# Random features of a linear-attention transformer computed as sixteen 32x32 TensorE tiles, with up and down pieces moved around them

## What is computed

```python
h = _layernorm(x) * (1 + ca) + sa
x = x + ga * attn_ref(h, ...)          # the first half of the kernel
h = _layernorm(x) * (1 + cb) + sb
return x + gb * ffn_ref(h, ...)        # the second half

def favor(x, omega):                   # dh = 16, m = 16, omega is 16 x 8
    xs = x * dh ** (-0.25)
    u = einsum('bshd,dm->bshm', xs, omega)
    h = 0.5 * sum(xs * xs, axis=-1, keepdims=True)
    return concatenate([exp(u - h), exp(-u - h)], axis=-1) * m ** (-0.5)

for l in range(3):                     # 16 heads of 16
    q, k, v = out @ Wq[l] + bq[l], out @ Wk[l] + bk[l], out @ Wv[l] + bv[l]
    Qf, Kf = favor(q, omega[l]), favor(k, omega[l])
    a = causal_linear_attention(Qf, Kf, v) @ Wo[l] + bo[l]
    h = layer_norm(out + a, ln1_g[l], ln1_b[l])
    y = relu(h @ W1[l] + bf1[l]) @ W2[l] + bf2[l]     # 256 -> 1024 -> 256
    out = layer_norm(h + y, ln2_g[l], ln2_b[l])
```

## Time and profile before

| | before |
|---|---|
| runs | 2620.6, 2623.1, 2625.83 us; median 2623.1 us |
| profiled execution | 2624.48 us, span of the instructions 2622.7 us |
| busy share of the span | PE 97%, DVE 81%, ACT 59%, POOL 54% |
| mean granted TensorE clock | 0.993 |
| chain that ended last | PE 90%, DVE 4%, issue 3%, ACT 2%, POOL 1% |

### The profile page before, as it was taken

The page is one execution under the profiler, slowest core; times in us unless marked ns, Lnnn a source line. Parts: engine busy times, 40 slices in busy tenths (PEclk is TensorE's granted clock), DMA queues, the critical chain, the costliest instruction groups (busy, mean ns, idle before and its releaser), DMA issues.

```text
span 2622.7 us, 63564 instructions
## 1 busy us (share of the span) xinstructions
PE 2545.6 (97%) x22368; PEld 2096.2 (80%) x22368; DVE 2119.8 (81%) x5244; ACT 1545.4 (59%) x3137; POOL 1423.9 (54%) x1406
## 2 busy tenths in 40 slices
PE   7899999999999999999898999999999999999998
PEld 4688888888888888887776788888888887888876
DVE  5788877887777787888899888878898887888775
ACT  3544455445544554455246777777777777776772
POOL 2244344443444345445476756656676666776664
PEclk9999999999999999999999999999999999999999
DMA  3100000010000010000111100000111100110001
GB/s 91 38 18 10 18 2 17 14 36 2 1 2 13 15 39 10 18 26 25 52 38 56 29 17 12 19 16 14 35 32 35 31 27 23 35 32 27 28 29 48
DMA packets 78985, 67.32 MB, mean 26 GB/s; under 512 B 15800, under 2 KB 73272, under 8 KB 78680
## 3 DMA queue, kind: packets, MB, share of 16 engines
q1 hardware_dynamic: 78680, 63.25, 8.1%
HBM read 49.18 MB, written 12.58 MB: 24 GB/s over the span
## 4 chain that ended last, share of the span: by engine, by line
PE 90%; DVE 4%; issue 3%; ACT 2%; POOL 1%; SPq 0%; DMA 0%; DVEq 0%; ACTq 0%; POOLq 0%
PE PS L274 79%; PE PS L984 4%; PE PS L946 1%; PE PS L1014 1%; PE PS L937 1%; PE PS L487 1%; PE PS L477 1%; PE PS L425 1%; PE PS L895 1%; DVE PS L3586 1%; DVE U L3178 1%; PE PS L1044 0%; ACT PR L2246 0%; DVE SQ L3566 0%; SPq L5388 0%
## 5 line engine op out<-in xcount | busy, mean ns | idle before, releaser
L2246 ACT ACTIVATE PR<-PS,SM 128x256 f32<-128x256 f32 (+1 forms) x512 | 280.3, 559 | 136.5 <-DVE SM L3591 136.0
L1932 ACT ACTIVATE FB<-PS,BC 128x512 f32<-128x512 f32 x192 | 133.4, 695 | 323.0 <-PE PS L274 184.7
L3178 DVE TENSOR_TENSOR U<-PS,CST 128x512 f32<-128x512 f32 x384 | 238.2, 683 | 34.2 <-PE PS L274 33.9
L4618 POOL TENSOR_TENSOR RL<-FB,RH 128x512 fp32r<-128x512 f32 x96 | 126.0, 1312 | 219.9 <-DVE RH L3155 219.9
L274 PE MATMUL PS<-W2H,RH 128*128 128x256 f32 x768 | 226.1, 294 | 6.7 <-POOL RL L4618 6.6
L4840 POOL TENSOR_TENSOR SM<-SM,COL 128x8 f32<-128x8 f32 x128 | 223.8, 1748 | 10.7
L3586 DVE CUSTOM_DVE_ANT_0 PS<-PS,MSK 128x256 f32<-128x256 f32 (+1 forms) x512 | 202.6, 436 | 29.4 <-PE PS L274 28.2
L274 PE MATMUL PS<-W2H,RL 128*128 128x256 f32 x768 | 215.9, 281 | 0.0
L274 PE MATMUL PS<-W2L,RH 128*128 128x256 f32 x768 | 215.8, 281 | 0.0
L4630 POOL TENSOR_TENSOR SBD<-SBD,TMP 128x256 f32<-128x256 f32 x84 | 64.3, 766 | 207.3 <-DVE TMP L3170 207.3
L274 PEld LDWEIGHTS PS<-W2H,RH 128*128 128x128 f32 x768 | 145.1, 189 | 29.5 <-issue 24.9
(11 more groups left out here) (265 smaller groups left out, 8535.6 us busy)
## 6 DMA issues: line engine op xcount, KB each, us to landing
PX<-in_L_attn_x SPq DMA_DIRECT2D x16, 512.0 KB, 3.6
TB<-in_k_rot SPq DMA_DIRECT2D x64, 128.0 KB, 2.1
SG<-in_L_attn_W SPq DMA_DIRECT2D x24, 256.0 KB, 2.7
xp_scratch<-PX SPq DMA_DIRECT2D x8, 512.0 KB, 2.9
xs_scratch<-X SPq DMA_DIRECT2D x64, 64.0 KB, 1.5
ZS<-xs_scratch SPq DMA_DIRECT2D x16, 256.0 KB, 2.8
GG<-xp_scratch SPq DMA_DIRECT2D x7, 512.0 KB, 3.8
out<-GG SPq DMA_DIRECT2D x7, 512.0 KB, 2.9
```

The lines of the kernel that those rows point to most:

```text
L1932: e.activation(FB[:, hb % 2, :], PS[:, 5, :], ACT.Relu, bias=BC[:, l % 2, 4 + hb:5 + hb]).then_inc(*a_re.up(n, hb))
L2246: t = e.activation(PR[:, par, 256 * i + lo:256 * i + hi], PS[:, 3 + par, 256 * i + lo:256 * i + hi], ACT.Exp, bias=S[:, 40 + 2 * g + i:41 ...
L3178: e.tensor_tensor(heads(U[:, u % 6, :], 4), heads(PS[:, g, :], 4), bcast(CM, 4), ALU.mult).then_inc(*d_mk.up(n, u))
L4618: e.tensor_tensor(RL[:, r, :], FB[:, 0, :], RH[:, r, :].bitcast(F), ALU.subtract).then_inc(*p_rl.up(n, hb))
```

## The change

Four things, all but the last in the first half:

1. **Layout.** Weights Wq and Wk are split into WQH and WQL in another order of columns (`places`), so that `proj(n, i)` gives four groups of 32 columns: two of queries, two of keys. The biases BC come in that order, in four transfers for a layer instead of two.
2. **Features.** `operands` is two instructions of 128 x 512 (numbers with bias in A, squares in B). `favor(n)` is one block of 32 matmuls of 32 x 32 weights: for each row group r and each of the four pairs c one with omega (OM) and, in a second round, one with the constant HO (CST) on the squares, into bank r at partitions 32c. It waits for all four pairs and both halves of the values. OM becomes 32 columns wide and loses its second GpSimd instruction.
3. **Order in steps 6 to 21 (and around `favor` elsewhere).** TensorE: values(n, 1) and up(m, 3) go ahead of the block, up(m, 4) directly behind it, down(m, 2) ahead of scores(n, 0). ScalarE: relu(m, 3) ahead of the exponents. VectorE: norm2_c ahead of add_bv(n + 1, 0), norm2_b behind add_bv(n, 1).
4. **Buffers.** Hidden block 0 of the second half gets its own G0, GG has five parts and QSB lies elsewhere. The scales of its first layer are loaded in the first half, those of the second layer at tile 4 of the second half, and `table` waits only for the layer that it needs.

```diff
     def split_parts(p):
+        if phase == 1 and at < 1024:
+            def places(w, k):
+                return w[:, 512 * k:512 * k + 512].rearrange("p (s t m f) -> p t m s f", s=4, t=2, m=2)[:, at // 512, :, :, :]
+            return [(places(WQH, k), places(WQL, k), s[:, 256 * k:256 * k + 256].rearrange("p (m s f) -> p m s f", m=2, s=4)) for k in range(2)]
...
-        def favor(n, i, bank):
-            e.wait_ge(*p_om.at(l, 1))
-            e.wait_ge(*a_sq.at(n, i))
-            if i < 2:
-                e.wait_ge(*a_sq.at(n, 2 + i))
-            else:
-                e.wait_ge(*d_v.at(n, i - 2))
-            mm(e, PS[0:64, bank, :], OM[:, l % 2, 0:64], OPS[i][0], True)
-            mm(e, PS[64:128, bank, :], OM[:, l % 2, 64:128], OPS[i][1], True).then_inc(*e_fv.up(n, i))
+        def favor(n):
+            e.wait_ge(*p_om.at(l))
+            for i in range(4):
+                e.wait_ge(*a_sq.at(n, i))
+            for i in range(2):
+                e.wait_ge(*d_v.at(n, i))
+            for r in BANKS:
+                for c in range(4):
+                    mm(e, PS[32 * c:32 * c + 32, r, :], OM[32 * r:32 * r + 32, l % 2, 0:32], OPS[c][0][32 * r:32 * r + 32, :], True)
+            for i, r in enumerate(BANKS):
+                for c in range(4):
+                    t = mm(e, PS[32 * c:32 * c + 32, r, :], HO[32 * r:32 * r + 32, 0:32], OPS[c][1][32 * r:32 * r + 32, :], False)
+                t.then_inc(*e_fv.up(n, i))
...
         def operands(n, i):
-            e.activation(A[lo, :], PS[lo, i, :], ACT.Identity, bias=col[lo, :])
-            e.activation(B[hi, :], PS[hi, i, :], ACT.Identity, bias=col[hi, :])
-            e.activation(A[hi, :], PS[lo, i, :], ACT.Square, bias=col[lo, :])
-            e.activation(B[lo, :], PS[hi, i, :], ACT.Square, bias=col[hi, :]).then_inc(*a_sq.up(n, i))
+            e.activation(A, PS[:, i, :], ACT.Identity, bias=col)
+            e.activation(B, PS[:, i, :], ACT.Square, bias=col).then_inc(*a_sq.up(n, i))
...
         for n in range(6, 22):             # ScalarE
             relu(m, 2)
+            relu(m, 3)
             features(n, 0, 2)
...
-            relu(m, 3)
...
         def table(u):
-                e.wait_ge(*t_qs.at(11))
+                e.wait_ge(*t_qs.at(11 if u >= 32 else 5))
...
         load_table(0)
-        load_scales(0)
-        load_scales(1)
         load_piece(P2 + 2)
```

More of the change, by code:

```diff
@@ L89, in build @@
     TB = sb("TB", [128, 2, 256])
-    QSB = sb("QSB", [128, 2, 256])
+    G0 = sb("G0", [128, 512])
     MSK = sb("MSK", [128, 384])
@@ L111, in build @@
     HTH, HTL = sb("HTH", [128, 2, 512], FR), sb("HTL", [128, 2, 512], FR)
-    GG = sb("GG", [128, 6, 512])
+    GG = sb("GG", [128, 5, 512])
+    QSB = sb("QSB", [128, 2, 256])
     PS = ctx.enter_context(nc.psum_tensor("PS", [128, 8, 512], F))
@@ L162, in build @@
     d_rh, d_rl = ev("d_rh", by(S24, R8)), ev("d_rl", by(S24, (1, 3, 5, 7)))
-    p_om = ev("p_om", by(range(3), R2))
+    p_om = ev("p_om", by(range(3)))
     p_xb, p_hb, p_al, p_zq = (ev(f"p_{k}", by(S24, R2)) for k in ("xb", "hb", "al", "zq"))
@@ L218, in build @@
     s_row = [ev(f"s_row{i}", by(range(3)), 16) for i in range(7)]
-    s_bb = ev("s_bb", by(range(3), range(11)), 16)
+    s_bb = ev("s_bb", by(range(3), range(13)), 16)
     s_x = ev("s_x", [("p", c) for c in S8] + [("r", n) for n in CH3], 16)
@@ L367, in hidden @@
     def hidden(q, hb):
-        return (KT, PR, PT)[hb // 2][:, hb % 2, :] if q == NQ - 1 else GG[:, hb, :]
+        return (KT, PR, PT)[hb // 2][:, hb % 2, :] if q == NQ - 1 else GG[:, hb - 1, :] if hb else G0[:, :]
     def rounded_hidden(q, hb):
@@ L375, in residual_of @@
     def residual_of(q):
-        return T2 if q == NQ - 1 else GG[:, 4:6, :]
+        return T2 if q == NQ - 1 else GG[:, 3:5, :]
     def gate_bank(q, hb):
@@ L428, in proj @@
         def proj(n, i):
-            m, nm = i % 2, "wk" if i < 2 else "wq"
             if n > 0:
                 e.wait_ge(*d_am.at(n - 1, 1))
-            need_weights(e, piece_of(n // 8, nm))
+            if i == 0:
+                need_weights(e, piece_of(n // 8, "wq"))
+                need_weights(e, piece_of(n // 8, "wk"))
             for k in range(2):
@@ L614, in _ @@
         values(0, 0)
+        values(0, 1)
         modulate(4)
         modulate(5)
[L617 to L621, removed]
+        favor(0)
         turn_k(0, 0)
@@ L710, in _ @@
         values(3, 0)
+        values(3, 1)
         up(1, 2)
[L712 to L716, removed]
+        favor(3)
         up(1, 3)
@@ L838, in _ @@
             down(m, 0)
+            values(n, 1)
             up(m, 2)
             down(m, 1)
[L841 to L845, removed]
             up(m, 3)
+            favor(n)
+            up(m, 4)
             attn_out(w, 0)
@@ L850, in _ @@
             turn_k(n, 1)
-            up(m, 4)
+            down(m, 2)
             scores(n, 0)
             key_sums(n)
-            down(m, 2)
             up(m, 5)
@@ L3360, in _ @@
         add_bv(3, 1)
+        norm2_b(0)
         running(3, 0)
@@ L3449, in _ @@
         add_bv(5, 1)
+        norm2_b(2)
         running(5, 0)
@@ L3536, in _ @@
             if n < 23: splits(n + 1, "a")
+            if n < 23 and m >= 0: norm2_c(m)
             if n < 23: add_bv(n + 1, 0)
-            if n < 23 and m >= 0: norm2_c(m)
         def low_x(u):
@@ L5363, in store_scaled, with load_scales @@
             e.dma_start(xp_d[4 * c:4 * c + 4].rearrange("t p d -> p t d"), PX.rearrange("p i (t d) -> p (i t) d", t=2)).then_inc(*s_xp.up(n))
+        def load_scales(l):
+            for i, nm in enumerate(("q", "k")):
+                v = ins[f"L0_ffn_{nm}_scale"][l:l + 1, :]
+                for z, (a, b, n) in enumerate(((0, 0, 64), (64, 32, 32), (96, 0, 32))):
+                    e.dma_start(QSB[:, 1 - l, 128 * i + a:128 * i + a + n], v[:, b:b + n].broadcast_to([128, n])).then_inc(*t_qs.up(6 * l + 3 * i + z))
+        load_scales(0)
         for n in range(16, 21):
@@ L5510, in constants @@
     sign = np.where(i % 16 < 8, 0.5, -0.5).astype(f)
-    other = (((i[:, None] + 64) % 128) // 16 == i[None, :] // 16).astype(f) * f(-0.125)
-    cst = np.stack([np.eye(128, dtype=f), blk, other, (i[:, None] <= i[None, :]).astype(f), blk * sign[None, :]], axis=1)
+    pairs = (i[:, None] % 32 // 16 == i[None, :] % 32 // 16).astype(f)
+    cst = np.stack([np.eye(128, dtype=f), blk, pairs * f(-0.125), (i[:, None] <= i[None, :]).astype(f), pairs * sign[None, :]], axis=1)
     c = np.arange(32)
```

72 lines of the change are left out of this document (24 added, 48 removed).

## The result

| | before | after |
|---|---|---|
| median, range (4 runs each) | 2621.85 us, 2620.16 to 2625.83 | 2665.94 us, 2664.67 to 2666.93 |
| ratio after / before, 95% interval | | 1.0166, 1.0148 to 1.0183 |
| span of the profiled execution | 2622.7 us | 2665.1 us |
| steps 6 to 21 | 845.95 us | 891.38 us |
| from the start of step 23 to the end | 1394.4 us | 1391.9 us |

A forecast was written before the change was run, and what follows sets the result against it. TensorE bounds the kernel, with no idle in steps 6 to 21. From the profiled 2624.5 us, +40 (loop), -7 (other steps), -9 (seam) and +16 (clock) give 2664.5, forecast as a median of 2663 us; range 2632 to 2698 us.

The forecast's parts named there:

- The mechanism: Steps 6 to 21: TensorE reaches down(m, 2) before GpSimd's RL is ready, then waits for VectorE's masks; +40 us.
- The block: Feature block: sixteen tiles run together, 2.0 us instead of 3.58 us, so 1.6 us less a step.
- The wait at down(m, 2): Steps 6 to 21: TensorE waits 3.0 us a step for GpSimd's RL, bounds 2.5 to 3.3 us.
- The masks: Waits for VectorE's masks: 0.8 us at sums(n, 0) and 0.3 us at the second sums, together 1.1 us a step.
- The sum of a step: Steps 6 to 21: 3.0 + 1.1 - 1.6 = 2.5 us more a step, without the clock.
- The clock: Steps 6 to 21: new idle lowers the granted clock, 1.4 us each in three steps of four, +16 us.
- The other eight steps and the seam: Outside steps 6 to 21: -7 us for the eight steps, -9 us for the seam between the halves.
- The faster one: Rival: RL is ready when TensorE reaches down(m, 2); 2599 us, or 2581 us with masks in time; chance 0.13.
- The one in which the forms cancel: Rival: wait of 1 to 2 us, no clock drop, within 0.2% of before; chance 0.05.
- Four tiles at a time: Rival: only four tiles run together in the feature block, which takes 6.9 us; about 2717 us, chance 0.06.

The follow-up runs named there:

- e1: Changed kernel with the old order of block, up(m, 3), up(m, 4), down(m, 2) and relu(m, 3) in steps 6 to 21; 2606.36 us, ratio 0.9919.
- e3: Changed kernel with low_hidden(m, 2) moved ahead of scale_queries(n, 0) on GpSimd in the loop; 2619.45 us, ratio 0.9975.
- e4: Kernel before, with 64-wide tiles and old seam, given only the loop's new order on TensorE, ScalarE and VectorE; 2709.11 us, ratio 1.0315.
- e8: e4 with relu(m, 2) moved ahead of the two casts of attention(w) on ScalarE; 2671.61 us, ratio 1.0172.
- e5: e1 with the first set of head scales issued late again, behind the first table between the halves; 2607.45 us, ratio 0.9927.
- e6: e5 with four added GpSimd tensor_tensor instructions of 128x256 beside VectorE's scans in steps 6 to 21; 2612.06 us, ratio 0.9947.
- e2: Changed kernel with only down(m, 2) moved back behind key_sums(n) in the loop; 2615.25 us, ratio 0.9957.

## Why the prediction was right, step by step

- **The mechanism held.** Down(m, 2) ahead of the scores outruns GpSimd's half of its hidden block, sixteen times, and the wait behind it at the sums is VectorE's. e1 to e3 each take the first one away and with it the loss.
- **The block:** 1.30 us less a step and not 1.6. Only the length differs (2.28 us for 2.0); sixteen tiles run at once. The trace's factor is 12. The estimate of 2.6 us by the factor of 10.6 of the Trainium skill ("TensorE: Matmul & The Clock Gate", Part 3) was 0.3 us too long, and my 2.0 us 0.3 us too short.
- **The wait at down(m, 2):** 2.02 us of idle, 2.27 us by TensorE's starts, and not 3.0. Two terms of the chain were too long. The scans take 2.46 us where I carried 3.23 over from the earlier trace rows (0.77 us); that row held a collision with GpSimd, and the change itself moves X0L out of its way. And FK starts 0.09 us ahead of the next piece's start, where I had it 0.14 us behind (0.23 us). GpSimd's two products take 0.14 us longer. Together that is the 0.9 us from 8.2 to 7.3 us behind the block. With the faster chain my lower bound of 2.5 us was too high.
- **The masks:** 0.65 us of idle, about 0.9 us by the starts, for 0.8. The 0.3 us at the second sums did not come. (The prediction's 2.82 less 2.1 us is 0.7, not 0.8, and its terms for the other eight steps add up to -7.6, not -7. Put right, the forecast would be some 2 us lower.)
- **The sum of a step:** +2.17 us without a drop, where I had +2.5; the terms measured make 1.9 (2.27 + 0.9 - 1.3), and 0.3 us of a step I can't place.
- **The clock:** nine drops at 1.2 us, +11, for twelve at 1.4, +16. e4 and e8 show the term as such: twelve drops went with a wait of 2.16 us and none with one of 1.00 us. Why seven of the sixteen steps with 2.0 us of idle have none stays open. It is not the length of the idle alone: behind the 3.0 us in step 23 the clock fell in e1, e5 and e6, and not in the changed kernel, e2 and e3.
- **The other eight steps and the seam** were summed 13 us too low. Steps 2 to 5 and 22 gave 2.2 us and step 1 gave 2.4, where I had some 6; the start and step 0 lost 4 us, of which the start's 1.9 us belongs to this one execution (step 0 begins at 20.1 us in it, and at 18.0 to 18.5 us in e1 to e3, whose start is the same; it alone has a stretch of 3.4 us at a clock of 0.50 from 14.5 us on). From step 23 to the end 2.5 us were gained and not 10: TB's landing took 7.1 us (1323.35 to 1330.47) where I took the scales' 4.8, and step 23 has the new wait of 2.99 us. I had covered the block's condition on the values for the loop, where three pieces stand between, and had not gone through it for step 23. In e1, where only two stand between, TensorE waits 2.05 us for it in step 10 of the loop as well (0.71 us there in e2 and e3, which keep the three).
- **Why the total fits nonetheless:** steps 6 to 21 cost 10.6 us less than I summed (45.4 for 56), the rest gave 13 us less than I summed. The sign and the place are understood; that the sum is 3 us off is partly luck.
- **The rivals.** The faster one had 2599 us if the wait at down(m, 2) isn't there, and 2581 us if the masks are in time too. e3 gives the first condition and takes 2619 us, e1 gives both and takes 2606 us: its prices were 20 and 25 us too low, some 12 and 13 us of it outside the loop. Its condition was not given in the changed kernel, where the chain takes 7.37 us and not 5.0. The one in which the forms cancel had a wait of 1 to 2 us and no clock drop; the wait was just above, and came with nine drops. Four tiles at a time is refuted by the rows of the block.

## What to carry to other kernels

Signals that used to come bank by bank come late when tiles are packed into one block: go through every engine's queue behind the last signal before work that needs its end is moved forward on the bottleneck. A duration from a trace holds only beside the same neighbours; look for what ran on the engine it shares an interface with. And where an order is written out in several places, price the new condition in each of them, since the loop's slack is not that of the last step.

## What the runs showed of the hardware

- Sixteen fp32 tiles of 32x32 with 512 columns run together: rounds 0.43 to 0.45 us apart, 2.28 us for 64 passes, factor 12 over one at a time.
- A VectorE scan of 128x512 or scalar_tensor_tensor of 128x256, and a GpSimd tensor_tensor, hold each other up when they overlap: the one that has to wait ends a fixed time behind the other. For the scan this is 1.08 us (1.28 us alone; 2.06 us in the kernel before, 1.74 and 1.57 us in e6), for scalar_tensor_tensor 0.28 us (0.48 us alone, 1.51 us in step 14 of the changed kernel), for GpSimd's 128x256 one 0.41 us (0.61 us alone, 1.41 us in e6).
- Idle of 2.0 to 2.2 us on TensorE brought the granted clock to 0.50 for 3.4 us in 9 and in 12 of sixteen steps; idle of at most 1.0 us, up to four times a step, brought it in none (e2, e3, e8). Such a drop cost 1.2 us in the changed kernel and 1.6 us in e4. Outside the loop idle of 3.0 us in step 23 brought it in three of six executions.
